# Issuing four row groups in turn, instead of two and two, in the score and maxima passes of a decoder kernel

## The reference

```python
# 32 heads of 32, L3_attn ("big")
dots = jnp.einsum('bhnd,bhmd->bhnm', q, k) * scale
attn = jax.nn.softmax(dots, axis=-1)
out  = jnp.einsum('bhnm,bhmd->bhnd', attn, v)
# 16 heads of 8 over 64 keys: L0_xattn (mask), L2_xattn (no mask), L3_xattn (mask)
scores = jnp.einsum('bhqd,bhkd->bhqk', Q, K) / sqrt(8)
attn   = softmax(scores)          # where the mask allows it
```

## Time and profile before

| | us |
|---|---|
| median of three runs | 1325.36 (1324.5 to 1325.76) |
| the profiled execution's own time | 1324.23 |
| span of the profile, first to last instruction | 1322.5 |
| VectorE busy | 912.4 (69%) |
| ScalarE busy | 691.6 (52%) |
| idle time of PE before L575, the largest of its own waits | 24.3 |

### The profile page before, as it was taken

One profiled execution on the slowest core, in us unless ns is written; L12 is line 12 of the kernel. 1 busy time (PEld: TensorE's weight loads), 2 busy tenths in 40 slices (PEclk: granted clock), 3 DMA queues, 4 the chain that ended last, 5 costly groups with the idle time before them and its releaser, 6 DMA issues. The chain is left out here.

```text
span 1322.5 us, 27373 instructions
## 1 busy us (share of the span) xinstructions
PE 1212.5 (92%) x10598; PEld 827.3 (63%) x10598; DVE 912.4 (69%) x2410; ACT 691.6 (52%) x1307; POOL 233.3 (18%) x337
## 2 busy tenths in 40 slices
PE   7779999999999999998998999989879999799885
PEld 4456767777777676775565676656556575566542
DVE  5563382465499968798976698866678766756466
ACT  2224464555554665345565646647426655377524
POOL 3320121212110130012201013011120112301122
PEclk8879999999999999999998999989989999999998
DMA  7001111211112100210000010000000000000000
GB/s 286 17 1 49 48 34 32 65 41 41 33 49 80 33 17 25 72 33 17 1 1 2 2 33 9 2 1 2 2 1 1 2 1 2 1 2 2 2 1 33
DMA packets 23287, 35.57 MB, mean 27 GB/s; under 512 B 4584, under 2 KB 12920, under 8 KB 22904
## 3 DMA queue, kind: packets, MB, share of 16 engines
q1 hardware_dynamic: 23160, 33.83, 8.1%
HBM read 32.77 MB, written 1.05 MB: 26 GB/s over the span
## 5 line engine op out<-in xcount | busy, mean ns | idle before, releaser
L2239 DVE TENSOR_REDUCE arena<-banks 128x4 f32<-128x1024 f32 x128 | 150.6, 1218 | 74.5 <-PE banks L2069 73.8
L1355 PEld LDWEIGHTS banks<-WE,arena 128*128 128x128 f32 x1536 | 180.0, 192 | 24.7 <-issue 22.6
L1355 PE MATMUL banks<-WE,arena 128*128 128x128 f32 x1536 | 182.7, 276 | 0.3 <-DVE R L1439 0.3
L1399 ACT ACTIVATE arena<-banks,BC 128x512 f32<-128x512 f32 x192 | 129.7, 690 | 99.9 <-PE banks L1339 99.4
L1339 PE MATMUL banks<-XT,WE 128*128 128x512 f32 x384 | 178.9, 602 | 0.0
L2219 ACT ACTIVATE arena<-banks 128x1024 f32<-128x1024 f32 x128 | 125.6, 1022 | 42.2 <-PE banks L2093 41.9
L1439 DVE SCALAR_TENSOR_TENSOR R<-banks,arena,R 128x128 f32<-128x128 f32 x256 | 72.0, 344 | 107.6 <-PE banks L1355 107.0
L613 ACT COPY arena<-banks 128x512 f32<-128x512 f32 x100 | 57.7, 589 | 120.7 <-PE banks L608 35.4
L1339 PEld LDWEIGHTS banks<-XT,WE 128*128 128x128 f32 x384 | 69.3, 193 | 66.3 <-issue 65.3
L2320 POOL TENSOR_TENSOR arena<-arena 128x256 f32<-128x256 f32 x56 | 43.0, 767 | 383.5 <-ACT arena L2201 383.5
L1902 DVE TENSOR_TENSOR arena<-arena 128x512 f32<-128x512 f32 x144 | 103.6, 719 | 0.0
(11 more groups left out here) (329 smaller groups left out, 2161.0 us busy)
## 6 DMA issues: line engine op xcount, KB each, us to landing
WE<-in_weights SPq DMA_DIRECT2D x64, 256.0 KB, 2.9
WE<-in_weights SPq DMA_DIRECT2D x64, 128.0 KB, 2.1
WS<-in_weights SPq DMA_DIRECT2D x1, 2368.0 KB, 13.0
RW<-in_rows SPq DMA_DIRECT2D x1, 1032.0 KB
XALL<-in_x SPq DMA_DIRECT2D x4, 256.0 KB, 10.1
out_dram<-arena SPq DMA_DIRECT2D x4, 256.0 KB, 2.3
WS<-in_weights SPq DMA_DIRECT2D x1, 900.0 KB, 7.7
WS<-in_weights SPq DMA_DIRECT2D x1, 645.0 KB, 7.8
```

The costliest lines, as they stand in the source:

```text
L1355: ins = PE.matmul(v[:, tile(t)], self.HT[:, e % 2, j, tile(t)], self.W[:, (8 * i + e) % RING, 1, j], start=j == 0, stop=j == self.J - 1)
L1399: A.activation(self.HT[:, e % 2, j], psum.view(f"{self.L}.h{i}.{e}.{j}"), ACT.Relu, bias=bcol(self.p + "_b1", e * self.J + j))\
L2239: V.tensor_reduce(big.mx[:, 2 * pair:2 * pair + 2], v, AX.X, ALU.max, negate=True).then_inc(dve.read(f"big.m{i}.{n}.{pair}"), 1)
```

## The change

In the four functions both pairs' banks are taken first, then the matmuls of the four row groups are issued in turn (row group 0, 1, 2, 3, and again), where before pair 0's were all issued ahead of pair 1's take and matmuls. The number, shapes and operands of the matmuls are the same, so is the order within a row group, and each pair still has its own increment on its last matmul. The waits on other engines' data stand behind both takes now. `scores` of the 32-head attention and `scores_pe` and `maxima_pe` of the others look like this after it:

```diff
             def scores(n):
                 pe.wait_ge(*psum.copied(f"big.hT{i}.{n}"))
-                for pair in range(2):
-                    v = psum.take(pe, f"big.e{i}.{n}.{pair}", 2)
-                    for hh in range(2):
-                        rows_of = row_group(2 * pair + hh)
-                        PE.matmul(v[:, hh].rearrange("p (a q) -> p a q", a=2), ones16[rows_of, :],
-                                  bc(big.HL[rows_of, n % 2], 1, 2), start=True, stop=True)
-                    for kt in range(2):
-                        for hh in range(2):
-                            rows_of = row_group(2 * pair + hh)
-                            ins = PE.matmul(v[:, hh, kt * S:kt * S + S], big.QK[rows_of, n % 3, S + kt * P:S + kt * P + P],
-                                            big.QK[rows_of, n % 3, 0:S], start=False, stop=True, skip_group_check=True)
-                    ins.then_inc(psum.filled(f"big.e{i}.{n}.{pair}"), 1)
+                v = [psum.take(pe, f"big.e{i}.{n}.{pair}", 2) for pair in range(2)]
+                for h in range(4):
+                    rows_of = row_group(h)
+                    PE.matmul(v[h // 2][:, h % 2].rearrange("p (a q) -> p a q", a=2), ones16[rows_of, :],
+                              bc(big.HL[rows_of, n % 2], 1, 2), start=True, stop=True)
+                for kt in range(2):
+                    for h in range(4):
+                        rows_of = row_group(h)
+                        ins = PE.matmul(v[h // 2][:, h % 2, kt * S:kt * S + S],
+                                        big.QK[rows_of, n % 3, S + kt * P:S + kt * P + P],
+                                        big.QK[rows_of, n % 3, 0:S], start=False, stop=True, skip_group_check=True)
+                        if kt == 1 and h % 2 == 1:
+                            ins.then_inc(psum.filled(f"big.e{i}.{n}.{h // 2}"), 1)
...
             def scores_pe(self, pe, i, b):
+                v = [psum.take(pe, f"{L}.s{i}.{b}.{pair}", 2) for pair in range(2)]
+                keep_awake(pe, f"{L}.s{i}.{b}", v[0][:, 0])
+                if b == 0:
+                    pe.wait_ge(*psum.copied(f"{L}.q{i}"))
+                pe.wait_ge(sig(L + ".km"), CB * i + b + 1)
+                pe.wait_ge(*psum.copied(f"{L}.hT{i}.{b}"))
+                for hp in range(2):
+                    for j in range(4):
...
+                    for j in range(4):
...
+                        if hp == 1 and j % 2 == 1:
+                            ins.then_inc(psum.filled(f"{L}.s{i}.{b}.{j // 2}"), 1)
...
             def maxima_pe(self, pe, i, b):
+                v = [psum.take(pe, f"{L}.m{i}.{b}.{pair}", 2) for pair in range(2)]
+                for t in range(2):
...
+                        for j in range(4):
...
```

More of the change, by code:

```diff
@@ L1007, in maxima_pe @@
                     pe.wait_ge(sig(L + ".fill"), i + 1)
-                for pair in range(2):
[L1009 to L1021, removed]
+                v = [psum.take(pe, f"{L}.m{i}.{b}.{pair}", 2) for pair in range(2)]
+                for t in range(2):
+                    if self.keep is not None:
+                        for j in range(4):
+                            of = row_group(j)
+                            PE.matmul(v[j // 2][:, j % 2, t * S:t * S + S].rearrange("p (n k) -> p n k", k=SK), ones16[of, :],
+                                      bc(self.fillr[of, b, :], 1, 4), start=True, stop=False)
+                    for j in range(4):
+                        of = row_group(j)
+                        ins = PE.matmul(v[j // 2][:, j % 2, t * S:t * S + S], self.QT16[of, tile(2 * b + t)],
+                                        self.KM16[of, b].rearrange("p h k -> p (h k)"),
+                                        start=self.keep is None, stop=True)
+                        if t == 1 and j % 2 == 1:
+                            ins.then_inc(psum.filled(f"{L}.m{i}.{b}.{j // 2}"), 1)
             def shifts_pe(self, pe, i, b):
@@ L1034, in scores_pe @@
                 L = self.L
[L1035 to L1053, removed]
@@ new lines, in scores_pe @@
+                v = [psum.take(pe, f"{L}.s{i}.{b}.{pair}", 2) for pair in range(2)]
[6 more added lines that the diff above has]
+                    for j in range(4):
+                        of = row_group(j)
+                        PE.matmul(v[j // 2][:, j % 2, hp * S:hp * S + S], pick_heads[of, hp].rearrange("p h k -> p (h k)"),
+                                  self.HL[of, b], start=True, stop=False)
+                    for j in range(4):
+                        of = row_group(j)
+                        ins = PE.matmul(v[j // 2][:, j % 2, hp * S:hp * S + S],
+                                        self.KM[of, b, 2 * hp:2 * hp + 2].rearrange("p h k -> p (h k)"),
+                                        self.QT[of, b * S:b * S + S], start=False, stop=True)
+                        if hp == 1 and j % 2 == 1:
+                            ins.then_inc(psum.filled(f"{L}.s{i}.{b}.{j // 2}"), 1)
@@ L2060, in maxima @@
             def maxima(n):
[L2061 to L2066, removed]
-                        for hh in range(2):
-                            rows_of = row_group(2 * pair + hh)
-                            ins = PE.matmul(v[:, hh, t * S:t * S + S], big.QK16[rows_of, n % 2, tile(t)],
-                                            big.QK16[rows_of, n % 2, S:2 * S], start=True, stop=True)
-                    ins.then_inc(psum.filled(f"big.m{i}.{n}.{pair}"), 1)
+                v = [psum.take(pe, f"big.m{i}.{n}.{pair}", 2) for pair in range(2)]
+                keep_awake(pe, f"big.m{i}.{n}", v[0][:, 0])
+                pe.wait_ge(sig("big.qk16"), GROUPS * i + n + 1)
+                for t in range(2):
+                    for h in range(4):
+                        rows_of = row_group(h)
+                        ins = PE.matmul(v[h // 2][:, h % 2, t * S:t * S + S], big.QK16[rows_of, n % 2, tile(t)],
+                                        big.QK16[rows_of, n % 2, S:2 * S], start=True, stop=True)
+                        if t == 1 and h % 2 == 1:
+                            ins.then_inc(psum.filled(f"big.m{i}.{n}.{h // 2}"), 1)
             def shifts(n):
```

## The result

The median of 20 runs went from 1324.72 us (1323.81 to 1327.55) to 1321.76 us (1320.16 to 1326.68); the ratio is 0.9978, 95% interval 0.997 to 0.9985. The change is worth 3.0 us, where 8.0 were forecast. The profiled execution took 1321.37 us, its span is 1319.7 us.

A forecast was written before the change was run, and what follows sets the result against it. PE, busy for 92% of the span, was taken to bound the kernel. 6.7 + 3.6 + 0.3 = 10.6 us, less 1.7 for the clock and 0.9 for stops, gave 8.0 us and 1317.4 us; range 1309 to 1325.

The forecast's parts named there:

- 37 free passes: 32-head score passes with pair 1 within 0.25 us of pair 0; 29 counted at 0.23 us, 6.7 us gained.
- 27 waiting passes, clock, stops: 32-head score passes waiting for banks gain 0, lose about 0.01 us each; clock costs 1.7 us, lengthened stops 0.9.
- 16-head score passes: 24 passes of the 16-head attentions; ten counted, nine of 0.34 us and one of about 0.5, 3.6 us gained.
- maxima passes: 88 maxima passes, both pairs starting together already; 0 to 0.03 us each, 0.3 us gained in all.
- A 32-head pass gets 0.23 us shorter: 32-head score pass: pair 1 starts with pair 0, so 1.42 us becomes 1.18 plus 0.01 for issuing.
- Four row groups can be kept going in turn: Products on PE: judged from the spread's 32 products, eight rounds of four in 1.89 us, 0.21 us a round.
- Pair 1 is held back by pair 0's instructions in the list, not by a bank: 32-head score pass: the bank is free at about 1196.88, PE arrives at 1197.00, pair 1 starts 0.24 us late.
- one clock stretch and 0.9 us: Emptier PE stops bring one more half-clock stretch, 1.7 us; stops that lengthen when PE arrives earlier cost about 0.9 us.
- Together 10.6 us taken out: Sum where PE bounds: 6.7 us from 32-head scores, 3.6 from 16-head scores, 0.3 from maxima.
- The slower rival: Empty stops before waiting passes bring more half-clock stretches, 1.7 us each, giving about 1329 us; chance 0.08.
- have their stretch already: PE's long stops are followed by a half-clock stretch already, so few are left to turn.
- Starts in program order: Matmuls on different row groups start strictly in list order; 56 us gained, about 1265 us; chance 0.02.

The follow-up runs named there:

- the free passes alone: New order only in the 37 32-head score passes whose second pair started within 0.25 us of the first, against the kernel before: 1315.65 us, 0.9938.
- a take between: 32-head scores only, against the kernel before: pair 1 taken after pair 0's ones and first halves, all second halves last: 1317.52 us, 0.9949.
- the early take in the old order: Both pairs' banks taken first in all four functions, matmuls in the old order, against the kernel before: 1331.72 us, ratio 1.0053.
- the second pair: Both score functions in the new order, against the 32-head scores alone in it, maxima as before: 1319.95 us against 1317.95.
- only the take moved: Both banks taken first in both maxima functions alone, matmuls in the old order, against the kernel before: 1330.02 us, 1.004.
- the stops filled: Full change with filler products between the takes of 25 waiting 32-head score passes: 1310.68 us; the same with the old maxima: 1311.26 us.
- the early take in the scores alone: Both banks taken first in the 32-head scores alone, matmuls in the old order, against the kernel before: 1328.24 us, 1.0033.
- seven passes: Kernel before with 4 to 9 filler products ahead of pair 0 in the seven longest-waiting 32-head score passes, against it without: 1314.28 us, 0.9927.

## Why the prediction was wrong, point by point

Four runs lead from the kernel before to the changed one: the free passes alone, the 32-head scores, both kinds of scores, the full change. Their steps, set against the terms of the sum, in us gained:

```
                                  forecast   by medians   by ratios
37 free passes                      6.7         9.8          8.2
27 waiting passes, clock, stops    -2.6        -2.3         -0.9
16-head score passes                3.6        -2.0         -2.7
maxima passes                       0.3        -1.8         -1.7
sum                                 8.0         3.7          2.9
```

The runs of a step aren't all of one set, so the medians add up to 3.7 and not to 3.0, and each step is uncertain by 2 to 3 us. Only the third is off by clearly more than that.

- *A 32-head pass gets 0.23 us shorter.* Right: 1.42 to 1.19. A group got 0.20 shorter, not 0.23: in the lonely stretches PE now comes to the scores 0.04 us before the bank is free. The prediction had named that margin (0.1 us) as a thing to watch.
- *Four row groups can be kept going in turn.* Right, but rows 6 was read too simply: nearly all of these products lie in a stretch at 0.50, so their 0.21 us a round is the pace at half clock. Float32 rounds at full clock take 0.22.
- *Pair 1 is held back by pair 0's instructions in the list, not by a bank.* Right: in the run with a take between, and in the changed kernel, it starts at once; with the early take in the old order it still starts 0.24 us late.
- *37 passes are free.* Right, each gives its 0.20 or 0.23 in the trace, and the run that changes only these gains 9.8 us (8.2 by the ratio). I had discounted eight of them and came to 6.7; the discount was too large.
- *16-head passes give 3.6 us.* This is the first step that failed, and the largest: "Ten are left, nine of 0.34 and one of about 0.5". The passes get shorter as forecast (1.54 to 1.21), but four comparisons give from 0.6 us gained to 2.0 lost: 1326.76 alone against 1325.18, 1319.95 against 1317.95, 1315.32 against 1315.65, 1311.26 against 1311.81. I took what ten passes lose in PE's list for what the kernel loses. In the traces of the second pair the gain is there up to 845 us and is gone by 890, where the kernel with it has 6.8 us more at 0.50. Why the stretches fall there, and whether the gain always goes that way, stays open.
- *The maxima passes give 0.3 us, and the earlier take costs one clock stretch and 0.9 us.* The second step that failed, in the maxima functions. "Queued behind it on PE is only the rest of the list, which waited for pair 1 anyway" looks at PE's list alone. What is queued behind pair 0 is on the other engines too: DVE's first reduce of the maxima, which frees the very banks that the scores' second pair waits for. For the score passes I followed that and came near: 2.6 us forecast, 2.3 measured. For the maxima passes I looked at the issue time (0 to 0.03 us) and never at their take, though one of them waited for ScalarE in the trace of before. They cost 1.8 us in the change, 3.4 alone, 4.0 with only the take moved, and nothing with the stops filled. Some of it is the chain shown above (1.3 us in one group), and in the traces of the maxima alone most of it goes with two stretches at 0.50.
- *Together 10.6 us taken out.* No run measures it: the 9.9 us between the early take alone and the full change also hold what the 27 waiting passes get back. If it is near at all, it is by luck. The discount on the free passes was too large by 3.1 us, and the 3.6 us of the 16-head passes aren't there.
- *More stretches at 0.50.* One appeared where it was expected, in the kernel with the early take in the scores alone. In the changed kernel's trace the sum between 600 and 1300 us is 51.2 us as before: some stretches are longer, some shorter. The slower rival had the mechanism and not the size.
- The long stops "have their stretch already", I wrote, and left them in the sum on both sides. That missed the largest thing in the profile: 10.9 us for seven passes.
- *Starts in program order.* Ruled out by the trace of after too: 5.15 us a group, not a microsecond less.

## What to carry to other kernels

Split a reordering into the order of the instructions and the order of the waits, and price the second on every engine that the delayed product feeds, for each function that is edited; the one in which the order gains nothing is where the wait is pure loss. When you measure one half alone, look whether it brings a delay of its own that the whole doesn't have: here 0.20 us in 27 passes were nearly all of what it seemed to cost. If two streams run side by side but one starts late, a reorder can gain only that lateness, and only where nothing else holds the late one. Where a wait of two or three microseconds has a stretch at half clock behind it, fill the wait first: it can be worth more than the schedule.

## What the runs showed of the hardware

- Matmuls on different row groups don't start in the order of the list: pair 1's ones start while six of pair 0's eight records are still to come. But they don't overtake at once; there it took 0.24 us, in the 16-head passes 0.35. In turn, four start within 0.013 us.
- Four row groups of float32 products in turn keep the pace of one: 16 records in 1.04 us with a tail of 0.37, four rounds of 0.22.
- Products that wait for nothing and are used by nobody, 52 in all, bring 10.9 us. In the trace the granted clock stays at 2.4 GHz behind them.
- The same kernel's executions differ by several us, and their granted clock with them: of 79 executions of the kernel before, 11 took 1315.8 to 1321.2 us at a mean granted clock of 0.963 to 0.969, the others 1323.2 to 1327.8 at 0.955 to 0.963. With the maxima alone changed it goes from 1318.7 to 1331.2 us. A difference of 2 us between two kernels here needs its interval read, and a trace shows one execution of that spread.
